# A table of places made row by row: 48 one-row comparisons in place of three broadcast ones

## The chip, the cores and the metric

The kernel runs on one core of one Trainium2 chip. The metric is the device time of one execution in microseconds (us). The core's engines are TensorE (PE; its weight loads are listed as PEld), VectorE (DVE), ScalarE (ACT), GpSimd (POOL) and SyncE (SP), which here only issues transfers.

## What is computed

A batch of 32 images is cut into 36 patches each and embedded; with a class token and 128 text tokens that makes 165 tokens of 256 features per image, 5280 tokens in all. One attention layer with 16 heads follows, then a mixture of experts in which every expert chooses its own tokens:

```python
xn = x_flat * rsqrt(mean(x_flat * x_flat) + EPS) * norm_weight
logits = xn @ router_w.T + router_b
probs = softmax(logits)
gates, idx = top_k(probs.T, cap)          # cap = 5280 / 8 = 660 tokens per expert
hmid = gelu(einsum('ech,efh->ecf', xn[idx], fc1_w) + fc1_b)
ye = einsum('ecf,ehf->ech', hmid, fc2_w) + fc2_b
out = zeros.at[idx].add(ye * gates) / max(gate sums, 1e-9)
```

## The kernel before, in words

The program runs attention over pairs of images (`round_of`), then finds each expert's 660th largest probability by a search on VectorE and ScalarE, numbers the chosen tokens (`POS`, from 0 to 659 per expert, negative where a token is not chosen), and runs the eight experts one after the other. All engines are programmed by hand, each with its own list of instructions; semaphores set the order between them. Within an engine the list is served in order.

**From a mask to a list of token numbers.** For one expert e the chosen tokens' slots lie on 110 partitions in `pos_t`, 48 columns (TPE = 3 groups k of 16). A slot number is split into a tile number a (0 to 5, six tiles of 110) and a place b (0 to 109) within the tile. `slots(e)` (lines 1464 to 1479) makes both: `GE` compares the slot with seven tile edges, `a_t` counts, `INA` is a 0/1 mark of the tile, and `b_t` is the slot less 110 times the tile number. `value_columns` (line 1486) multiplies five value columns (two that make the token number, three that make its weight) by `INA` into `RHS`. `one_hot_places(e, parts)` (lines 1496 to 1504) makes `ONEB`, a table of 48 blocks of 110 numbers in bfloat16: block i of partition p is 1 at the place b_t[p, i] and 0 elsewhere. One part k is 16 blocks. TensorE then multiplies each of the 48 blocks with the matching `RHS` columns and sums them in PSUM (`slot_values`, line 1106; for expert 0 `first_tokens`, line 1087, and `first_weights`, line 1095), which gives the token number and weight of every slot. `tokens(e)` turns that into indices; POOL gathers the rows of those tokens by indirect transfers (line 597).

**One expert on TensorE** (lines 1183 to 1202). `fc1` (line 1142) multiplies in three passes (high and low parts), 16 pieces of 6 matrix multiplications; piece n waits until VectorE has split the hidden piece n-3 (`h_ready`). `fc2` (line 1162) makes four quarters of 24. Between them stand `expert_transposes` (line 1121) of the next expert's gathered rows, `output_rows` (line 1176) and, after fc1's second piece (expert 0: its eighth), `slot_values(e + 1)`, which waits for all of the table: `pe.wait_ge(oh_ready, (NK + 1) * (e + 1))`.

**One expert on VectorE** (`expert`). For expert 0: part 0 of table 1, the low part of hidden piece 2 (`low_hidden`, line 1589), part 1, pieces 3 and 4, part 2, then the rest. For every expert e while e + 2 < 8: after the hidden pieces come the low parts of the next W1 (line 1573), `one_hot_values(e + 2)`, two of `low_xeT(e + 1)` (line 1581), part 0 of table e + 2, `weigh` of three output tiles (line 1567), two more of `low_xeT`, and parts 1 and 2 of table e + 2. Then the next expert's `hidden` begins (lines 1599, 1589, 1602). The table of expert 0 is made ahead of all that, straight after the search. ScalarE makes the hidden pieces (lines 776, 778). POOL scatters weighted rows (line 610).

The table `ONEB` is stored in `H`, `b_t` in an arena (`R_ARENA`) that many short-lived tiles share.

Of the kernel before, what the change touches and what calls it, by code (L numbers as in the profile page):

```python
# [8 lines left out]
BF16 = mybir.dt.bfloat16  # L9
U32 = mybir.dt.uint32  # L10
I32 = mybir.dt.int32
ALU = mybir.AluOpType
# [26 lines left out]
SEG = 128 // NE  # L39
SEGT = NTOK // SEG  # L40
A = 110
# [3 lines left out]
TPE = NK * SEG  # L45
# [80 lines left out]
def build(nc, xT, wl, h0, addrows, clsrows, minus, watt, vecs, rowv, w1, w2, const_f, const_b, out):  # L126
    ctx = ExitStack()
    with ctx:  # L128
        def sb(name, shape, dt=F32):
            return ctx.enter_context(nc.sbuf_tensor(name, shape, dt))  # L130

        def sem(name):
            return ctx.enter_context(nc.semaphore(name))
# [11 lines left out]
        def kb(name):  # L145
            return cb[:, CB[name][0]:CB[name][1]]
# [26 lines left out]
        def cut(arena, *shape, dt=F32):  # L173
            n = int(np.prod(shape))
            words = n if dt == F32 else n // 2
            v = arena[:, at[0]:at[0] + words]
            at[0] += words
            assert at[0] <= arena.shape[1], at[0]
            if dt != F32:
                v = v.bitcast(dt)  # L180
            if len(shape) > 1:
                names = "abcde"[:len(shape)]
                v = v.rearrange(f"p ({' '.join(names)}) -> p {' '.join(names)}", **dict(zip(names, shape)))
            return v

        ONEB = cut(H, TPE, A, dt=BF16)
# [4 lines left out]
        R_ARENA = sb("r_arena", [128, 8576])  # L191
# [23 lines left out]
        GE = cut(R_ARENA, TPE, NA + 1, dt=BF16)  # L215
        INA = cut(R_ARENA, TPE, NA, dt=BF16)
        a_t = cut(R_ARENA, TPE)
        b_t = cut(R_ARENA, TPE, dt=BF16)
        SGN = cut(R_ARENA, ONACT, SEGT)
        at[0] = 4 * 4 * T + 2 * KD * PAIR + KD * T + 3 * RT * D + KD * PAIR  # L220
        VAL = cut(R_ARENA, NCOL, NV + 1, dt=BF16)
        slotv = cut(R_ARENA, NTB, NV, NA)
# [84 lines left out]
        oh_ready, idx_done, tok_chain, tok_ready = [sem(n) for n in ("oh_ready", "idx_done", "tok_chain", "tok_ready")]  # L307
# [316 lines left out]
        def _(act):  # L624
# [112 lines left out]
            for step in range(STEPS):  # L737
# [6 lines left out]
                for c in range(ONACT):  # L744
                    act.activation(SGN[:, c, :], R[:, :], ACT.Sign, bias=here[:, NCAND - ONACT + 1 + c:NCAND - ONACT + 2 + c],
                                   scale=-1.0, accum_out=cnt[:, NCAND - ONACT + c:NCAND - ONACT + c + 1]).then_inc(cnt_act, 1)
# [460 lines left out]
        def _(dve):  # L1207
# [286 lines left out]
                value_columns(e, RHS, 0, NV, oh_ready)  # L1494

            def one_hot_places(e, parts=range(NK)):
                iota = kb("iota")[0:A, :].rearrange("p (o a) -> p o a", o=1).to_broadcast([A, SEG, A])
                if e == 1:
                    dve.wait_ge(idxw_done, 1)
                for k in parts:  # L1500
                    place = b_t[0:A, k * SEG:(k + 1) * SEG].rearrange("p (s o) -> p s o", o=1)\
                        .to_broadcast([A, SEG, A])
                    dve.tensor_tensor(ONEB[0:A, k * SEG:(k + 1) * SEG, :], place, iota, ALU.is_equal)\  # L1503
                       .then_inc(oh_ready, 1)

            def gate_weights():
                link(dve.scalar_tensor_tensor(gate[0:A, :], pos_t[0:A, :], 0.0, pr_t[0:A, :], ALU.is_ge, ALU.mult))
# [97 lines left out]
            def expert(e, u, seen, more):  # L1605

                v = 1 - u
                if e == 0:
                    one_hot_places(1, range(0, 1))
                    low_hidden(0, range(2, 3))  # L1610
                    one_hot_places(1, range(1, 2))
                    low_hidden(0, range(3, 5))
                    one_hot_places(1, range(2, 3))
                    low_hidden(0, range(5, 2 * SV_AT_FIRST + 2))
                    tokens(1)
                    low_hidden(0, range(2 * SV_AT_FIRST + 2, 2 * KFF))
                else:
                    hidden(e, u, seen, range(0, 1))
                    weigh(e - 1, range(3, NA))
                    hidden(e, u, seen, range(1, SV_AT + 1))  # L1620
                    tokens(e + 1)
                    hidden(e, u, seen, range(SV_AT + 1, KFF))
                low_W1(e + 1, v)
                if more:
                    one_hot_values(e + 2)
                low_xeT(e + 1, range(0, 2))
                if more:
                    one_hot_places(e + 2, range(0, 1))
                weigh(e, range(0, 3))
                low_xeT(e + 1, range(2, 4))  # L1630
                if more:
                    one_hot_places(e + 2, range(1, NK))
# [72 lines left out]
```

## Time and profile before

| | |
|---|---|
| runs of the kernel | 847.13, 850.50, 850.14 us; median 850.14 |
| the profiled execution | 851.15 us, of which the span from first to last instruction is 849.4 us |
| granted TensorE clock, mean over the span | 0.927 of full speed |
| TensorE busy | 745.9 us (88%) |
| VectorE busy | 567.9 us (67%), 1343 instructions |
| ScalarE, GpSimd busy | 396.9 us (47%), 378.0 us (45%) |
| span from the search's end to the end | from about 538 us on |

An engine's busy time is the time in which an instruction of it was under way. Durations of consecutive VectorE instructions can overlap: the interval from start to start is then shorter than the duration of one. A merged row of the timeline ("x3") gives the time from the first one's start to the last one's end, so the interval is (that time less one duration) over (count less one). In a chain of waits each row is a stretch on the path that ended last.

### The profile page before, as it was taken

The numbers are of one execution on the slowest core, as the hardware profiler recorded it, in microseconds if no ns is written. First come the engines' busy times: TensorE is split into PE (matmuls) and PEld (weight loads), VectorE is DVE, ScalarE is ACT, GpSimd is POOL, SyncE is SP. The second block draws the span as 40 slices with busy tenths as digits, with TensorE's granted clock in tenths as the row PEclk, the third lists the DMA queues.
The fourth block names the chain that finished last, engine by engine and source line by source line (L and its number), as shares of the span: only waits on it lengthen the run. The fifth ranks groups of instructions, "written<-read, shape, count | busy, mean of one in ns | idle before, by whom it ended". The sixth has DMA issues, their size and how long they took to land. (4 is left out here: it accounts for less than half of the span.)

```text
span 849.4 us, 18757 instructions
## 1 busy us (share of the span) xinstructions
PE 745.9 (88%) x6840; PEld 674.8 (79%) x6840; DVE 567.9 (67%) x1343; ACT 396.9 (47%) x857; POOL 378.0 (45%) x526
## 2 busy tenths in 40 slices
PE   3699999999999999999998521379999999999994
PEld 2577888888888888888887421369999999999994
DVE  1135777677677687677675267785787787877561
ACT  0213454554454554554542247045547466375570
POOL 3113454554554554554543326023636437355334
PEclk8899999999999999999998655569999999999998
DMA  9963666546865666656653161112344443442122
GB/s 297 288 97 47 92 107 93 91 103 98 123 104 97 90 102 99 121 102 97 88 94 74 35 217 64 40 30 82 38 133 79 104 141 53 129 98 35 35 30 32
DMA packets 80687, 82.37 MB, mean 97 GB/s; under 512 B 36161, under 2 KB 74943, under 8 KB 80244
## 3 DMA queue, kind: packets, MB, share of 16 engines
q1 hardware_dynamic: 67980, 66.92, 39.6%
q0 software_dynamic: 11584, 10.96, 8.0%
q10 hardware_dynamic: 1032, 3.30, 1.1%
q8 instruction: 55, 0.90, 0.5%
q14 instruction: 36, 0.29, 0.1%
HBM read 34.59 MB, written 16.22 MB: 60 GB/s over the span
## 5 line engine op out<-in xcount | busy, mean ns | idle before, releaser
L610 POOL DMA_INDIRECT out<-r_arena x48 | 80.3, 1674 | 118.3 <-DVE r_arena L1567 106.3
L523 POOL TENSOR_SCALAR_AFFINE_SELECT r_arena<-r_arena 126x660 f32<-126x660 f32 x128 | 97.0, 768 | 52.6 <-ACT r_arena L671 52.3
L671 ACT ACTIVATE r_arena<-ps_all 126x660 f32<-126x660 f32 x128 | 92.2, 720 | 59.0 <-PE ps_all L899 57.4
L1273 DVE TENSOR_REDUCE mx<-ps_all 128x4 f32<-128x504 f32 (+1 forms) x160 | 105.0, 669 | 16.1 <-PE ps_all L876 14.8
L1284 DVE RECIPROCAL r_arena<-ps_all 128x165 f32<-128x165 f32 x64 | 76.1, 1189 | 57.4 <-PE ps_all L914 57.4
L876 PE MATMUL ps_all<-Kp,Qp 96*65 96x56 f32 (+1 forms) x512 | 91.7, 295 | 0.0
L1589 DVE TENSOR_TENSOR hT_lo<-r_arena,hT_hi 128x330 fp32r<-128x330 f32 x128 | 63.4, 501 | 40.2 <-ACT r_arena L778 39.8
L899 PE MATMUL ps_all<-Qp,Kp 98*126 98x166 f32 x512 | 85.3, 290 | 4.4 <-ACT r_arena L671 2.9
L597 POOL DMA_INDIRECT xe<-xn_rows,r_arena x48 | 59.5, 1240 | 59.7 <-issue 35.7
L776 ACT ACTIVATE hT_hi<-ps_all,vec_s 128x330 fp32r<-128x330 f32 x128 | 68.9, 538 | 35.9 <-PE ps_all L1142 33.8
L1142 PE MATMUL ps_all<-xeT_hi,W_hi 128*128 128x330 f32 x256 | 83.4, 326 | 1.1 <-DVE xeT_lo L1581 1.1
L1142 PE MATMUL ps_all<-xeT_lo,W_hi 128*128 128x330 f32 x256 | 82.7, 323 | 0.0
L649 ACT ACTIVATE q_hi<-ps_all,vec_s 128x166 fp32r<-128x166 f32 x64 | 22.0, 395 | 129.6 <-PE ps_all L837 129.6
L1142 PE MATMUL ps_all<-xeT_hi,W_lo 128*128 128x330 f32 x256 | 82.1, 321 | 0.0
L1162 PE MATMUL ps_all<-hT_hi,W_hi 128*128 128x330 f32 x256 | 81.7, 319 | 0.0
L1162 PE MATMUL ps_all<-hT_hi,W_lo 128*128 128x330 f32 x256 | 80.8, 315 | 0.0
L1162 PE MATMUL ps_all<-hT_lo,W_hi 128*128 128x330 f32 x256 | 80.4, 314 | 0.0
L899 PEld LDWEIGHTS ps_all<-Qp,Kp 98*126 98x126 f32 x512 | 69.7, 192 | 10.4 <-ACT r_arena L671 6.4
L876 PEld LDWEIGHTS ps_all<-Kp,Qp 96*65 96x65 f32 (+1 forms) x512 | 67.9, 168 | 5.6
L778 ACT ACTIVATE r_arena<-ps_all,vec_s 128x330 f32<-128x330 f32 x128 | 68.0, 532 | 0.0
L914 PE MATMUL ps_all<-r_arena,V 126*32 126x165 f32 x1024 | 61.6, 313 | 1.1 <-POOL r_arena L523 1.0
L914 PE MATMUL ps_all<-r_arena,cf 126*32 126x165 f32 x1024 | 60.2, 307 | 0.0
(178 smaller groups left out, 1703.7 us busy)
## 6 DMA issues: line engine op xcount, KB each, us to landing
H<-w SPq DMA_DIRECT2D x16, 1024.0 KB, 6.0
Qp<-q_hi SPq DMA_DIRECT2D x64, 166.0 KB, 3.9
Kp<-k_hi SPq DMA_DIRECT2D x128, 63.0 KB, 4.2
Qp<-q_lo SPq DMA_DIRECT2D x32, 166.0 KB, 4.7
out<-H SPq DMA_DIRECT2D x16, 330.0 KB
xn_rows<-r_arena SPq DMA_DIRECT2D x16, 330.0 KB
Kp<-k_lo SPq DMA_DIRECT2D x64, 63.0 KB, 4.1
H<-h SPq DMA_DIRECT2D x1, 3360.0 KB, 25.5
```

The source lines that it names most:

```text
L523: pool.affine_select(PT[0:S, g, :, :], PT[0:S, g, :, :], [[0, 4], [STEP - 1, T]], ALU.is_ge, 0.0, base=STEP - 2, channel_multiplier=-STEP) ...
L610: pool.indirect_dma_start(rows_out, bass.IndirectOffsetOnAxis(tok[0:A, e % NTB, a:a + 1], 0), yw[0:A, a, :], None, bounds_check=NTOK - 1, ...
L671: act.activation(PT[0:S, g, :, :].rearrange("p (k h) t -> p k h t", k=2), pair[:, :, :, 0:T], ACT.Exp, scale=float(HD) ** -0.5).then_inc(e ...
L776: act.activation(hT_hi[:, f, j * HALF:(j + 1) * HALF], bank(n % 4)[:, 0:HALF], ACT.Gelu, bias=b1_s[:, e, f:f + 1]).then_inc(gelu_done, 1)
L778: act.activation(h_raw[:, n % 4, :], bank(n % 4)[:, 0:HALF], ACT.Gelu, bias=b1_s[:, e, f:f + 1]).then_inc(gelu_done, 1)
L876: mm = pe.matmul(dst[0:rows, 2 * j * cols:2 * (j + 1) * cols].rearrange("p (w s) -> p w s", w=2), Qp[0:MROW, q, h, at_row:at_row + rows], ...
L899: mm = pe.matmul(dst[0:S, j * TE:(j + 1) * TE], Kp[0:MROW + 2, q, h, g % 2, :], Qp[0:MROW + 2, q, h, :], start=(j == 0), stop=(j == 1), sk ...
L914: mm = pe.matmul(dst, lhs, PT[0:S, 2 * c + w, j, :], start=(w == 0 and part == 0), stop=(w == 1), skip_group_check=True)
L1142: mm = pe.matmul(bank(n % 4)[:, 0:HALF], w[:, k, f * 128:(f + 1) * 128], x[:, k, cols], start=(i == 0), stop=(i == len(terms) - 1))
L1162: mm = pe.matmul(bank(4 + c)[:, 0:HALF], w[:, f, c * 128:(c + 1) * 128], h[:, f, cols], start=(i == 0), stop=(i == len(terms) - 1))
L1273: dve.tensor_reduce(dst, src, AX.X, ALU.max).then_inc(max_ready, 1)
L1284: dve.reciprocal(rS[:, c, :], bank(2 + c)[:, T:2 * T]).then_inc(rs_sum, 1)
```

## The change

`one_hot_places` issues, for each block i, one `tensor_scalar` over 110 numbers that compares the row 0 to 109 with the number in `b_t[:, i]` of each partition (a per-partition scalar operand), in place of one `tensor_tensor` per part over 16 blocks, in which both the places and the row 0 to 109 are spread by a step of 0. The semaphore is raised by the last of each 16. `b_t` becomes float32, and it is cut from the arena after `SGN` instead of before.

```diff
         a_t = cut(R_ARENA, TPE)
-        b_t = cut(R_ARENA, TPE, dt=BF16)
         SGN = cut(R_ARENA, ONACT, SEGT)
+        b_t = cut(R_ARENA, TPE)
@@
             def one_hot_places(e, parts=range(NK)):
-                iota = kb("iota")[0:A, :].rearrange("p (o a) -> p o a", o=1).to_broadcast([A, SEG, A])
                 if e == 1:
                     dve.wait_ge(idxw_done, 1)
                 for k in parts:
-                    place = b_t[0:A, k * SEG:(k + 1) * SEG].rearrange("p (s o) -> p s o", o=1)\
-                        .to_broadcast([A, SEG, A])
-                    dve.tensor_tensor(ONEB[0:A, k * SEG:(k + 1) * SEG, :], place, iota, ALU.is_equal)\
-                       .then_inc(oh_ready, 1)
+                    for i in range(k * SEG, (k + 1) * SEG):
+                        ins = dve.tensor_scalar(ONEB[0:A, i, :], kb("iota")[0:A, :], b_t[0:A, i:i + 1], None, ALU.is_equal)
+                    ins.then_inc(oh_ready, 1)
```

## Rows read from the trace of the kernel before

**Rows 1.** Chain of waits, experts 0 and 1: start us, us, what.

```profile
570.09 0.44 ACT r_arena L778
570.55 0.50 DVE hT_lo L1589
571.06 1.91 DVE H L1503
573.01 2.69 PE ps_all L1106 x48
...
603.51 2.41 PE ps_all L1106 x48
605.92 12.88 PE ps_all L1142 x84
```

**Rows 2.** TensorE's waits after 573 us: waiter, released by: us, times, longest.

```profile
PE ps_all L1106 <- DVE H L1503: 0.9, 1, 0.9
```

**Rows 3.** The table's line by itself: duration ns min/median/max, first and last start.

```profile
L1503 DVE TENSOR_TENSOR H<-r_arena,cb x24: 1979/1982/1991, 540.9 to 771.7; 110x1760 bf16<-110x1760 bf16 x24
```

**Rows 4.** Timeline, table of expert 0: start us, us, engine, line, operation.

```profile
540.86 5.79 DVE L1503 TENSOR_TENSOR H<-r_arena,cb 110x1760 bf16<-110x1760 bf16 x3
546.70 1.66 PE L1087 MATMUL ps_all<-RHS,H 110*110 110x12 bf16 x16 [0.25 <-DVE H L1503]
```

**Rows 5.** Timeline of VectorE, table of expert 1.

```profile
565.64 1.99 DVE L1503 TENSOR_TENSOR H<-r_arena,cb 110x1760 bf16<-110x1760 bf16 x1
567.69 0.50 DVE L1589 TENSOR_TENSOR hT_lo<-r_arena,hT_hi 128x330 fp32r<-128x330 f32 x1
568.11 1.99 DVE L1503 TENSOR_TENSOR H<-r_arena,cb 110x1760 bf16<-110x1760 bf16 x1
570.01 1.04 DVE L1589 TENSOR_TENSOR hT_lo<-r_arena,hT_hi 128x330 fp32r<-128x330 f32 x2
```

**Rows 6.** Timeline, table of expert 2 and TensorE's pass over it.

```profile
593.66 1.98 DVE L1503 TENSOR_TENSOR H<-r_arena,cb 110x1760 bf16<-110x1760 bf16 x1
596.61 1.27 DVE L1567 TENSOR_SCALAR r_arena<-ps_all,r_arena 110x256 f32<-110x256 f32 x3 [0.96 <-PE ps_all L1176]
598.61 3.88 DVE L1503 TENSOR_TENSOR H<-r_arena,cb 110x1760 bf16<-110x1760 bf16 x2
...
603.35 2.57 PE L1106 MATMUL ps_all<-RHS,H 110*110 110x30 bf16 x48
```

**Rows 7.** VectorE rows for the fixed part of an instruction, without and with a per-partition scalar.

```profile
26.16 0.33 DVE L1313 COPY bvB<-vec_s 128x110 f32<-128x110 f32 x2
...
L1313 DVE COPY bvB<-vec_s 128x110 f32<-128x110 f32 x2 | 0.3, 208 | 0.0
...
528.42 0.55 DVE L1388 TENSOR_SCALAR_CACHE_REDUCE r_arena<-r_arena,cand 128x330 f32<-128x330 f32 x1
...
528.89 0.55 DVE L1388 TENSOR_SCALAR_CACHE_REDUCE r_arena<-r_arena,cand 128x330 f32<-128x330 f32 x1
...
L1567 DVE TENSOR_SCALAR r_arena<-ps_all,r_arena 110x256 f32<-110x256 f32 x48 | 20.2, 477 | 21.9 <-PE ps_all L1176 14.1 <-issue 7.8
```

**Rows 8.** VectorE rows for the rate: elements per cycle.

```profile
L1455 DVE TENSOR_SCALAR r_arena<-r_arena 128x330 f32<-128x330 f32 x1 | 0.3, 333 | 0.0
L1454 DVE TENSOR_TENSOR r_arena<-r_arena 128x330 f32<-128x330 f32 x1 | 0.5, 502 | 0.0
...
L1474 DVE TENSOR_TENSOR r_arena<-r_arena 110x288 bf16<-110x288 bf16 x8 | 2.6, 324 | 0.0
```

**Rows 9.** Windows: us, engines' busy time, PEclk, DMA share, GB/s.

```profile
572.08:575.40 3.32, 2.39 (x48) 2.39 (x48) 2.12 (x4) 1.17 (x3) 0.00 (x0) 1.00 0.00 0
575.40:578.80 3.40, 3.40 (x17) 3.40 (x16) 0.06 (x1) 0.96 (x2) 0.00 (x0) 0.50 0.00 0
...
592.00:838.00 246.00, 245.37 (x1856) 244.65 (x1855) 181.12 (x403) 140.86 (x295) 120.17 (x81) 1.00 0.36 80
```

**Rows 10.** A VectorE copy beside GpSimd's transfers: duration ns min/median/max.

```profile
L1599 DVE CAST W_hi<-H x56: 280/286/389, 602.4 to 821.9; 128x256 fp32r<-128x256 f32 x56
```

## The prediction, made before the changed kernel was run

> **What bounds the kernel now.** I read the chain of waits first, in order of time, for the stretch in which the table is used, then TensorE's list of waits, then the timelines around the table. From 573 us to 837 us the chain is TensorE alone, pass after pass, with one wait by the list [rows 2]: 0.9 us before the pass over the table of expert 1. Ahead of it stands VectorE's last part of that table [rows 1]. So the 21 parts for experts 1 to 7 cost the kernel nothing but that wait, while the three for expert 0, made with TensorE idle, lie on the path in full. The table takes 24 instructions of 1.98 us [rows 3]. What matters is, first, whether 16 one-row comparisons are shorter or longer than one broadcast one, and second, how much room the table has before TensorE wants it.
>
> **Interval of the old instruction.** Three parts take 5.79 us, one lasts 1.98 us: (5.79 - 1.98) / 2 = 1.905 us from start to start [rows 3, 4]. Per element VectorE takes (1982 - 502) / (1760 - 330) = 1.035, say 1.04 ns at one element per cycle [rows 3, 8]; 1760 elements are 1830 ns, so 75 ns of the interval are fixed and the broadcast form runs at one element per cycle.
>
> **Interval of the new one.** It has two terms, and neither shape is in the trace.
>
> Fixed part. Without a per-partition scalar it is 65 to 75 ns: two copies of 110 elements take 0.33 us, one lasts 208 ns, so 122 ns from start to start, less 57 ns for 110 elements at two per cycle [rows 7]. With such a scalar, two quite different instructions give the same larger value: L1388 starts every 0.47 us with 330 elements (470 - 343 = 127 ns), and three L1567 take 1.27 us with one of 477 ns, so 396 ns each, less 256 x 1.04 = 266 ns, is 130 ns [rows 6, 7]. The scalar costs some 60 ns that the preceding instruction doesn't hide. Bounds: 65 and 130 ns. I take 130, since it is what both rows with a scalar show; neither row is exactly of this form (one also reads out an accumulator, the other reads PSUM).
>
> Streaming part. A float32 `tensor_scalar` within SBUF lasts 333 ns where the two-source one of the same 330 elements lasts 502: 169 ns less, half of the 343, so two per cycle [rows 8]. Two 16-bit sources of 288 elements last 324 ns, which is 150 ns fixed and 174 ns of streaming, near two per cycle too [rows 8]. The new instruction has one source within SBUF and 16-bit elements on both sides, so both doublings should apply: 110 x 1.04 / 4 = 29 ns. Bounds: 29 ns, 57 ns at two per cycle, 115 ns at one.
>
> I take 130 + 29 = 159 ns from start to start, and 211 + 29 = 240 ns for the duration (L1567 has 477 - 266 = 211 ns outside its stream). Sixteen take 16 x 0.159 = 2.54 us against 1.905. Each part is 0.64 us longer: the stream shrinks from 1.83 to 0.46 us, but the fixed parts grow from 0.075 to 2.08 us.
>
> The Trainium skill, Vector Engine (DVE) Microarchitecture Reference, section Measured stream behaviour on trn2, speaks against this: built-in ops pay about 75 ns per instruction after queue overlap, and it names no extra for a scalar. By that rule sixteen would take 16 x (75 + 29) ns = 1.66 us and the change would gain a little; the rows agree with 75 ns for instructions without such a scalar and have 127 to 130 for those with one.
>
> **Where it lands, place by place.**
>
> Expert 0's table. Before, it begins at 540.86 us and ends at 546.65. After, the last of 48 ends at 540.86 + 47 x 0.159 + 0.24 = 548.57: **+1.9 us**, all on the path; TensorE's pass over each part (1.66 us) stays shorter than a part and only the last shows [rows 4].
>
> Expert 1's table. Part 0 starts at 565.64 and ends its turn at 568.18 instead of 567.55; hidden piece 2 was ready at about 567.69, so part 1 starts at 568.60 instead of 568.11, ends its turn at 571.14, pieces 3 and 4 take 2 x 0.42 us (before they waited for ScalarE, whose rows end at 570.53), and part 2 runs from 571.98 to 571.98 + 15 x 0.159 + 0.24 = 574.60 instead of 572.96 [rows 1, 5]. TensorE waits for exactly this: **+1.6 us**, and its idle stretch grows from 0.9 to about 2.6 us. The hidden pieces behind part 2 are late as well, but they are wanted after a table pass of 2.4 us.
>
> Tables of experts 2 to 7 (six times the same pattern, 34.2 us apart; the first is in the rows). Part 0 starts at 593.66 and would end at 596.2; `weigh` behind it waits for TensorE until 596.61 anyway, so that one is free (0.96 us idle before, 0.3 after). Parts 1 and 2 start at 598.61; the last of 32 ends at 598.61 + 31 x 0.159 + 0.24 = 603.78, and TensorE wants the table at 603.35 [rows 6]. With 0.05 us for the signal that is a new wait of 0.48 us, six times: **+2.9 us**. The point from which this begins is an interval of (603.35 - 0.05 - 0.24 - 598.61) / 31 = 0.144 us; the cover of 0.9 us is used up. Queued behind on VectorE are the W2 split, hidden pieces 0 and 1 and `weigh` of three more tiles: 1.3 us late, but the hidden piece that VectorE needs next comes only after TensorE's table pass of 2.4 us [rows 1], so it catches up, and fc1 wants none of these rows before that pass is over.
>
> Everything else. The number of semaphore raises stays; TensorE's passes read the same bytes; `b_t` as float32 is 48 elements of one short instruction per expert, made well ahead: nothing.
>
> **TensorE's clock.** After its wait of 0.93 us and its pass over the table the granted clock was 0.50 for 3.40 us, that is 1.2 instead of 2.4 GHz, and those 3.4 us did the work of 1.7: 1.7 us lost. In the 246 us after, where the same pass comes without a wait, the clock stays at 1.00 [rows 9]. The change lengthens the first wait and puts a shorter one (0.48 us) in front of six other passes. Bounds: no further fall, or one at each of the seven, 0 to 11.9 us. New waits are half as long as the one that was followed by a fall, so I take one further fall: **+1.7 us**.
>
> **The sum.** 1.9 + 1.6 + 2.9 + 1.7 = 8.1 us. The profiled execution took 851.15 us (span 849.4), so it would take 859.3. It lies 1.0 us above the median of the runs, 850.14, on which I put the forecast: **858.3 us**.
>
> **GpSimd.** Its indirect transfers run beside the table. The Trainium skill, SBUF — State Buffer, in its part on ports, says that a VectorE instruction in a two-port mode keeps GpSimd out of SBUF for its whole length, and that whichever comes first holds up the other. A two-per-cycle copy runs 56 times in this stretch, some beside such transfers, and lasts 280 to 389 ns with a median of 286 [rows 10], so the trace shows at most 0.1 us for one of 56: I put it at zero.
>
> **The rivals.**
>
> A, the scalar is free (chance 0.14). The interval is 70 + 29 = 99 ns, 1.58 us per part. Expert 0's table then waits for TensorE's own passes (three of 1.66 us) and gains 0.8 us; expert 1's part 2 still starts at 570.97, held by ScalarE, and gains 0.3; the rest is covered. 850.1 - 1.1 = 849.0 us, no slower than before. For it: every row without a scalar. Against it: both rows with one. It decides below 119 ns (1.905 / 16).
>
> B, the faster stream fails by half (0.12). Two elements per cycle, because only one of the doublings applies. Interval 187 ns, duration 270: +3.3, +3.0 and six waits of 1.4 us, 14.8 us in all: 864.9 us. No row has both doublings at once. At one per cycle (0.04) the interval is 245 ns: +6.1, +5.8, part 0 delays `weigh` by 1.0 us, and six waits of 4.2 us give 37 us: 887 us.
>
> C, the clock (0.10). The waits come out as forecast, but the clock falls behind nearly each: 6.4 + 6 x 1.7 = 16.6, 866.7 us. For it: the one fall behind a wait; against it: the new waits are half as long.
>
> **How the numbers follow.** The forecast has 0.60, and by itself a range of 852 to 862: 852 if the interval is just under the 0.144 us at which the six waits go, 862 with three falls. The range for 8 in 10 leaves out A and the one-per-cycle case: 851 to 867. Half a percent, 4.25 us, is about what a measurement here can tell from no change: slower than 854.4 are B, C and nearly all of the forecast, 0.80; within it A and the forecast's low end, 0.18; faster by more, 0.02.
>
> **What would show it.** In the changed kernel's trace: 384 one-row comparisons of about 240 ns (180 with no price for the scalar, 268 at two per cycle), merged groups of 16 or 32 that take 0.159 us each; TensorE's first pass over expert 1's table about 3.5 us later than before; in its list of waits, seven on the table, one of 2.6 us and six of 0.5; the clock row after 592 us below 1.00 if there were falls. The forecast is wrong if the interval is below 0.144 us or the six waits are missing.

## The result and the profile after

The changed kernel takes 861.47 us (median of 4 runs, 861.01 to 861.66) against 850.07 for the kernel before on the same chip: 1.015 times as long, 95% interval 1.012 to 1.018, so 11.4 us slower. Forecast were 858.3 us and a range of 851 to 867. Measured again on another chip (below) it was 865.07 against 848.44, so 16.6 us slower.

The profiled execution has a span of 859.9 us. The table's line, by itself and in the timeline; columns as in [rows 3] and [rows 4 to 6].

```profile
L1501 DVE TENSOR_SCALAR H<-cb,r_arena x384: 233/246/610, 536.8 to 784.4; 110x110 bf16<-110x110 bf16 x192
...
564.09 2.64 DVE L1501 TENSOR_SCALAR H<-cb,r_arena 110x110 bf16<-110x110 bf16 x16 [0.29 <-DVE r_arena L1536]
566.65 0.50 DVE L1587 TENSOR_TENSOR hT_lo<-r_arena,hT_hi 128x330 fp32r<-128x330 f32 x1
567.06 2.64 DVE L1501 TENSOR_SCALAR H<-cb,r_arena 110x110 bf16<-110x110 bf16 x16
569.61 0.90 DVE L1587 TENSOR_TENSOR hT_lo<-r_arena,hT_hi 128x330 fp32r<-128x330 f32 x2
570.43 2.63 DVE L1501 TENSOR_SCALAR H<-cb,r_arena 110x110 bf16<-110x110 bf16 x16
...
595.29 2.63 DVE L1501 TENSOR_SCALAR H<-cb,r_arena 110x110 bf16<-110x110 bf16 x16
598.23 1.27 DVE L1565 TENSOR_SCALAR r_arena<-ps_all,r_arena 110x256 f32<-110x256 f32 x3 [0.30 <-PE ps_all L1176]
...
600.23 5.24 DVE L1501 TENSOR_SCALAR H<-cb,r_arena 110x110 bf16<-110x110 bf16 x32
```

(2.64 - 0.246) / 15 is 0.160 us from start to start, so a part takes 2.55 us instead of 1.905. Part 0 of table 2 still ends ahead of the weighing (L1565), which waits 0.30 us where it waited 0.96 [rows 6]; parts 1 and 2 end 5.24 us after their start instead of 3.88.

TensorE's list of waits from 573 us on, where before there was one of 0.9 us [rows 2]:

```profile
PE ps_all L1106 <- DVE H L1501: 4.2, 7, 1.8
```

The longest of the seven stands in front of the pass over table 1. Some microseconds ahead of it TensorE waits once more, for a hidden piece:

```profile
570.16 0.42 PE L1142 MATMUL ps_all<-xeT_hi,W_hi 128*128 128x330 f32 x1 [0.79 <-DVE hT_lo L1587]
...
573.12 3.91 PE L1106 MATMUL ps_all<-RHS,H 110*110 110x30 bf16 x48 [1.79 <-DVE H L1501]
```

The chain of waits over two experts:

```profile
636.64 3.29 DVE H L1501 x21
639.95 1.85 DVE H L1501 x11
641.80 0.04 issue
641.85 2.61 PE ps_all L1106 x48
644.46 13.09 PE ps_all L1142 x84
...
674.94 1.94 DVE H L1501 x11
676.93 2.61 PE ps_all L1106 x48
679.54 14.42 PE ps_all L1142 x84
```

Before, the chain was TensorE alone in this stretch and fc1's 84 multiplications took 12.88 us [rows 1]. Now VectorE's table is on it in each of the six experts, and fc1 behind the pass takes 13.1 and 14.4 us in turn. The 14.4 us are the clock's doing: it is low for part of the stretch behind the first, third and fifth pass, 0.63 of full speed on the mean of the window below; the windows (columns as in [rows 9]) show it behind the pass over table 2 and not behind that over table 3:

```profile
609.00:612.50 3.50, 3.50 (x17) 3.50 (x17) 0.50 (x1) 1.82 (x4) 2.89 (x3) 0.63 0.39 37
644.30:657.40 13.10, 13.10 (x89) 12.91 (x88) 9.30 (x30) 11.50 (x26) 10.62 (x8) 1.00 0.37 61
```

**Where the time went.** The stage begins with VectorE's copy of the slots (line 1459). Attention and search ahead of it are untouched, but vary from run to run: over the thirteen traces of this study the copy starts between 532.3 and 540.6 us. So the cleaner comparison is from that copy to the end of the span. It is still one execution of each kernel, and the clock in expert 0 differs between executions by up to 2.7 us (see e6). The kernel before:

```profile
L1459 DVE COPY r_arena<-ps_all x1: 558/558/558, 538.2 to 538.2; 110x384 f32<-110x384 f32 x1
```

The changed one:

```profile
L1459 DVE COPY r_arena<-ps_all x1: 558/558/558, 534.1 to 534.1; 110x384 f32<-110x384 f32 x1
```

From there it is 849.4 - 538.2 = 311.2 us before and 859.9 - 534.1 = 325.8 after: 14.6 us more. In these two executions the part ahead of the stage was 4.1 us shorter in the changed kernel, so that the spans differ by 10.5 only; the medians differ by 11.4, on the second chip by 16.6. The 14.6 us, from milestone to milestone:

| from | to | before | after | more |
|---|---|---|---|---|
| copy of the slots | token numbers of expert 0 | 10.2 | 12.1 | 1.9 |
| token numbers of expert 0 | pass over table 1 | 24.6 | 26.9 | 2.3 |
| pass over table 1 | pass over table 2 | 30.3 | 32.4 | 2.1 |
| five times: pass to next pass | | 171.2 | 179.2 | 8.0 |
| pass over table 7 | end | 74.9 | 75.2 | 0.3 |

### The profile page after: what moved, and what is told of

The parts are those of the page before. It is cut to its first block and busy times, and to the rows that moved or that the text cites. A ratio compares the mean times of both kernels' runs of the same rounds, so it can differ in the third digit from the quotient of the medians.

```text
span 859.9 us, 19117 instructions
## 1 busy us (share of the span) xinstructions
PE 749.4 (87%) x6840; PEld 677.1 (79%) x6840; DVE 583.2 (68%) x1703; ACT 398.0 (46%) x857; POOL 374.6 (44%) x526
## 5 line engine op out<-in xcount | busy, mean ns | idle before, releaser
L610 POOL DMA_INDIRECT out<-r_arena x48 | 77.1, 1606 | 127.4 <-DVE r_arena L1565 115.4
L1273 DVE TENSOR_REDUCE mx<-ps_all 128x4 f32<-128x504 f32 (+1 forms) x160 | 104.8, 668 | 15.4 <-PE ps_all L876 14.1
L1142 PE MATMUL ps_all<-xeT_hi,W_hi 128*128 128x330 f32 x256 | 86.0, 336 | 1.9 <-DVE xeT_lo L1579 1.1
L1142 PE MATMUL ps_all<-xeT_lo,W_hi 128*128 128x330 f32 x256 | 85.0, 332 | 0.0
L1142 PE MATMUL ps_all<-xeT_hi,W_lo 128*128 128x330 f32 x256 | 84.4, 330 | 0.0
L1501 DVE TENSOR_SCALAR H<-cb,r_arena 110x110 bf16<-110x110 bf16 x384 | 63.0, 268 | 0.3 <-DVE r_arena L1536 0.3
```

Source lines behind the costliest of these rows:

```text
L610: pool.indirect_dma_start(rows_out, bass.IndirectOffsetOnAxis(tok[0:A, e % NTB, a:a + 1], 0), yw[0:A, a, :], None, bounds_check=NTOK - 1, ...
L1142: mm = pe.matmul(bank(n % 4)[:, 0:HALF], w[:, k, f * 128:(f + 1) * 128], x[:, k, cols], start=(i == 0), stop=(i == len(terms) - 1))
L1273: dve.tensor_reduce(dst, src, AX.X, ALU.max).then_inc(max_ready, 1)
L1501: ins = dve.tensor_scalar(ONEB[0:A, i, :], kb("iota")[0:A, :], b_t[0:A, i:i + 1], None, ALU.is_equal)
```

## The experiments

Each time stands against the kernel before, run on the same chip (its medians there: 848.21 us for e1 to e4, 848.44 for e5 to e8, 849.07 for e9 to e11). e1 is not in the table: its own time, 859.82 us, says nothing. "Stage" is the length from the copy of the slots to the end in the profiled execution, 311.2 us for the kernel before.

| kernel | median us | ratio, 95% interval | stage us |
|---|---|---|---|
| e2, table 0 by rows | 850.94 | 1.0029 (0.9998 to 1.0060) | 313.7 |
| e6, table 1 by rows | 852.34 | 1.0053 (1.0029 to 1.0077) | 317.1 |
| e3, tables 2 to 7 by rows | 855.96 | 1.0094 (1.0061 to 1.0127) | 320.0 |
| e4, two of three parts of tables 2 to 7 | 849.41 | 0.9997 (0.9975 to 1.0019) | 311.1 |
| e5, the change again | 865.07 | 1.0198 (1.0157 to 1.0240) | 326.9 |
| e7, the change, SV_AT 2 | 857.22 | 1.0088 (1.0053 to 1.0124) | 319.4 |
| e9, broadcast form, tables 2 to 7 delayed | 857.70 | 1.0093 (1.0067 to 1.0119) | 322.0 |
| e11, the change, SV_AT 2 and SV_AT_FIRST 5 | 854.05 | 1.0053 (1.0016 to 1.0090) | 314.4 |
| e10, the kernel before, SV_AT_FIRST 5 | 846.97 | 0.9971 (0.9949 to 0.9993) | 309.3 |
| e8, table in pairs | 922.42 | 1.0865 (1.0828 to 1.0902) | 386.0 |

**e1, series of single instructions.**

```diff
+for i in range(16): tensor_scalar(ONEB[:, i], row, a_t[:, i:i+1], is_equal)          # 1
+for i in range(16): tensor_scalar(ONEB[:, i], row, 5.0, is_equal)                    # 2
+for i in range(8):  tensor_scalar(sgn[i*A:(i+1)*A], ones[0:A], a_t[:, i:i+1], is_equal)   # 3, float32
+for i in range(4):  tensor_scalar(flat[880 numbers], cb[0:880], a_t[:, i:i+1], is_equal)  # 4
+for i in range(4):  tensor_scalar(flat[880 numbers], cb[0:880], 5.0, is_equal)       # 5
+for i in (1, 2):    tensor_tensor(cells(i), b_t spread over 110 rows of 16, cells(0), is_equal)  # 6
```

> The kernel before, with series of instructions put in between the search and the first table, where VectorE works alone; they write scratch, and the whole run is longer by their sum (about 16 us), so its time says nothing. Series 1: 16 one-row comparisons of 110 bf16 with a float32 scalar per partition. Series 2: the same with a constant in the instruction. Series 3: 8 of 110 float32 with a scalar per partition. Series 4 and 5: 4 of 880 bf16, with a scalar per partition and with a constant. Series 6: 2 two-source comparisons of 1760 bf16 in which the innermost step of both sources is one. Theory 'the scalar per partition costs 60 ns, the stream runs at four per cycle': from start to start 160, 100, 190, 360 and 300 ns in series 1 to 5. Rival 'fixed part of 100 ns plus two per cycle, and the scalar is free': 160, 160, 160, 560 and 560 ns. Series 6: 0.99 us if two per cycle, 1.9 us if one.

The timeline of VectorE, and below it each line's durations in ns (min/median/max):

```profile
535.68 2.63 DVE L1641 TENSOR_SCALAR H<-cb,r_arena 110x110 bf16<-110x110 bf16 x16
538.35 1.67 DVE L1644 TENSOR_SCALAR H<-cb 110x110 bf16<-110x110 bf16 x16
540.05 1.58 DVE L1647 TENSOR_SCALAR r_arena<-cf,r_arena 110x110 f32<-110x110 f32 x8
541.67 1.52 DVE L1650 TENSOR_SCALAR H<-cb,r_arena 110x880 bf16<-110x880 bf16 x4
543.23 1.28 DVE L1653 TENSOR_SCALAR H<-cb 110x880 bf16<-110x880 bf16 x4
544.55 2.06 DVE L1656 TENSOR_TENSOR H<-r_arena,H 110x1760 bf16<-110x1760 bf16 x2
...
L1641 DVE TENSOR_SCALAR H<-cb,r_arena x16: 241/244/253, 535.7 to 538.1; 110x110 bf16<-110x110 bf16 x16
L1644 DVE TENSOR_SCALAR H<-cb x16: 186/188/195, 538.4 to 539.8; 110x110 bf16<-110x110 bf16 x16
L1650 DVE TENSOR_SCALAR H<-cb,r_arena x4: 444/444/449, 541.7 to 542.8; 110x880 bf16<-110x880 bf16 x4
```

Series 1 starts every (2.63 - 0.244) / 15 = 159 ns, series 2 every (1.67 - 0.188) / 15 = 99: the scalar per partition costs 60 ns of the engine's time. Series 4 starts every (1.52 - 0.444) / 3 = 359 ns; 770 elements more take 200 ns more than in series 1, 0.26 ns each, so the stream does run at four per cycle. Series 3 and 5 start every 187 and 300 ns (by their lines' medians of 271 and 381 ns). The theory is right on all six; the rival meets only series 1. (The sum was overestimated: 11 us, not 16.) The Trainium skill's 75 ns per instruction (Vector Engine (DVE) Microarchitecture Reference, Measured stream behaviour on trn2) is met by series 2, 99 - 29 = 70 ns; series 1 has 130, which that page doesn't mention. Series 6 starts every 2.06 - 1.07 = 0.99 us: the two-source comparison runs at two per cycle once no innermost step is 0.

**e2, table 0 alone; e6, table 1 alone; e3, tables 2 to 7 alone.** In each, a table is made by rows or as before:

```diff
+            def by_rows(e, k):
+                return e == 0            # e6: e == 1; e3: e >= 2
...
+                    if by_rows(e, k):
+                        for i in range(k * SEG, (k + 1) * SEG):
+                            ins = dve.tensor_scalar(ONEB[0:A, i, :], kb("iota")[0:A, :], b_r[0:A, i:i + 1], None, ALU.is_equal)
+                        ins.then_inc(oh_ready, 1)
+                        continue
```

> Only the table of expert 0 by rows, all others in the broadcast form. Theory 'each table costs what the chain says': table 0 lies on the path in full, +1.9 us over the kernel before, about 852, plus or minus a change of the clock in expert 0. Rival 'the loss of 11 us is set off by the late start of expert 0 (other clock, other order of transfers)': most of the 11 us comes with this alone, about 860.

> Only the table of expert 1 by rows. Theory: TensorE's wait in front of this table grows by 1.6 us, and the clock falls for longer after it (up to 1.7 us): +1.6 to +3.5 us. Rival 'the hidden pieces behind the table hold up TensorE too': a second wait behind the table pass, +4 us or more.

> Only the tables of experts 2 to 7 by rows, those of 0 and 1 in the broadcast form. Theory 'six waits in front of the table pass, and what the clock makes of them': six waits of 0.4 to 0.5 us (2.9 us) and two or three falls of the clock (1.4 us each), in all +6 to +8 us, about 857. Rival 'the steady part costs only its waits': +3 us, 853.

Measured +2.7, +3.9 and +7.8 us by the medians, +2.5, +5.9 and +8.8 by the stage. The rival that the late start of expert 0 sets off everything is out: table 0 alone gives 2.7 us. So is e6's rival: no wait for a hidden piece stands behind the pass over table 1.

Of the 5.9 us of e6's stage, 2.7 arise ahead of the first row comparison. The clock stood at 0.50 all the way from expert 0's token numbers to that comparison, and TensorE's 48 multiplications for expert 0's weights took 4.42 us instead of 2.40. The chain and the window of e6, then the chain of the kernel before:

```profile
557.42 4.42 PE ps_all L1096 x48
542.50:562.40 19.90, 11.11 (x75) 10.72 (x76) 14.40 (x34) 3.49 (x8) 6.95 (x6) 0.50 0.12 34
```

```profile
562.59 2.40 PE ps_all L1095 x48
```

In the kernel before the clock had risen by then (0.68 on the mean from 556.0 to 565.6 us). From the token numbers to the start of table 1 it is 19.9 us in e6 and 17.3 in the kernel before, although nothing there is by rows. The trace of e9, whose table 1 is in the broadcast form, has the same: its pass over table 1 starts 2.7 us later after the token numbers. Why the clock rises late in some executions is open. Without these 2.7 us table 1 costs 3.2 by the stage, within the theory's 1.6 to 3.5, and the median's interval (2.5 to 6.5 us) doesn't speak against it. The three parts then add up to 2.5 + 3.2 + 8.8 = 14.5 us, against 14.6 for the whole change.

Of the 3.2 us, 1.7 are the later start of the pass (its wait is 1.8 us instead of 0.93). The other 1.5 lie behind it, where the clock is low for longer, as the windows from the start of the pass over table 1 show. The kernel with table 1 by rows:

```profile
571.49:574.99 3.50, 3.50 (x47) 3.50 (x47) 1.17 (x3) 0.00 (x0) 0.00 (x0) 0.65 0.00 0
574.99:586.49 11.50, 11.50 (x66) 11.50 (x66) 4.69 (x13) 8.20 (x17) 3.47 (x4) 0.81 0.08 22
```

The kernel before:

```profile
573.01:576.51 3.50, 3.50 (x52) 3.50 (x52) 1.19 (x3) 0.24 (x1) 0.00 (x0) 0.84 0.00 0
576.51:588.01 11.50, 11.50 (x70) 11.50 (x70) 5.81 (x15) 9.31 (x18) 4.45 (x4) 0.90 0.11 32
```

That is (0.35 x 3.5 + 0.19 x 11.5) - (0.16 x 3.5 + 0.10 x 11.5) = 1.7 us of full-speed work lost more.

TensorE's list of waits of the kernel with tables 2 to 7 by rows:

```profile
PE ps_all L1107 <- DVE H L1507: 2.4, 6, 0.5
```

Six waits of 0.4 us make 2.4 us. In its chain the clock falls behind three of the six passes, as many as in both traces of the change, but not the same ones: here behind the first, second and fifth.

**e4, two of three parts by rows.**

```diff
-                return e >= 2
+                return e >= 2 and k < 2
```

> In the tables of experts 2 to 7, parts 0 and 1 by rows and part 2 broadcast; tables 0 and 1 broadcast. 192 of the 384 one-row comparisons are there. Theory 'there is cover for 0.9 us behind the weighing and for 0.96 us ahead of it': part 0 is 0.65 us later and hidden, part 1 is 0.65 us later and hidden, so no wait of TensorE on these tables, no fall of the clock after 592 us, and the time of the kernel before, 850. Rival 'every one-row comparison costs its share wherever it stands' (by contention on VectorE's side): half of the loss, 855.

849.41 us, 0.9997 of the kernel before. The timeline of VectorE and TensorE's list of waits over experts 1 to 7:

```profile
593.54 1.27 DVE L1576 TENSOR_SCALAR r_arena<-ps_all,r_arena 110x256 f32<-110x256 f32 x3 [0.29 <-PE ps_all L1177]
...
595.54 2.68 DVE L1507 TENSOR_SCALAR H<-cb,r_arena 110x110 bf16<-110x110 bf16 x16
598.14 1.98 DVE L1512 TENSOR_TENSOR H<-r_arena,cb 110x1760 bf16<-110x1760 f32 x1
...
PE ps_all L1107 <- DVE H L1512: 0.9, 1, 0.9
```

192 one-row comparisons, which cost VectorE 12 x 0.65 = 7.8 us more, cost the kernel nothing: the only wait left is that on table 1. So the row form costs nothing where there is cover for it; a second late part in a row has none.

**e9, no row form, only the delay.**

```diff
+                    if e >= 2 and k == 2:
+                        dve.tensor_tensor(idle, b_t[0:11] spread, iota spread, ALU.is_equal)   # 1210 elements of scratch
                     place = b_t[0:A, k * SEG:(k + 1) * SEG]
```

> The kernel before, all tables in the broadcast form; in the tables of experts 2 to 7 a scratch comparison of 1210 elements stands in front of part 2, so that parts 1 and 2 end 1.3 us later, as they do by rows. No one-row comparison is in it. Theory 'the loss of tables 2 to 7 comes from when the table is ready, and from the clock that falls behind the wait': six waits of 0.4 to 0.5 us, two or three falls of the clock after 592 us, and the time of the kernel with only these tables by rows, +8 us, 856. Rival 'it comes from the one-row comparisons themselves, from two-port accesses against GpSimd for one': +3 us or less, 851.

857.70 against 849.07 us: +8.6, where the row form of the same tables costs 7.8. (2.7 us of its stage in the table above stand ahead of table 1's pass, see e6.) This is the test that settles the steady part: the loss comes from when the table is ready. TensorE's waits in it, table 1's among them:

```profile
PE ps_all L1106 <- DVE H L1509: 3.1, 7, 1.0
```

That is some 2.1 us in the six, and again three falls of the clock, behind the first, second and fifth pass.

**e5, the change again; e7, the pass over the table later; e11, both passes later.**

```diff
-SV_AT, SV_AT_FIRST = 1, 4
+SV_AT, SV_AT_FIRST = 2, 4            # e7; e11: 2, 5
```

> The changed kernel once more, for its time beside the kernel before on this chip and a second look at where its clock falls. If the losses add up (table 0, table 1, tables 2 to 7): 2.5 + about 2.5 + 8 = 13 us over the kernel before. Rival 'they share something, so that the sum is less': 8 to 10 us.

> The changed kernel with SV_AT 2 instead of 1: from expert 1 on TensorE takes the table pass two pieces of fc1 later, so 1.8 us more cover; VectorE reads the pass's result one round of hidden pieces later. All 384 comparisons stay by rows. Theory 'the eight us of tables 2 to 7 come from the waits in front of the pass': the six waits go, no fall of the clock after expert 1, and about 8 us come back: 4 to 5 us over the kernel before. Rival 'they come from VectorE being busier everywhere': at most 3 us come back.

> The changed kernel with SV_AT 2 and SV_AT_FIRST 5: both passes two pieces later. With SV_AT 2 alone it took 857.2 us, 8.8 over the kernel before. Theory 'the fast form of the table is late for expert 1 by 2.6 us, of which 1.8 us can be covered': 2 to 4 us less than with SV_AT 2 alone, 853 to 855. Rival 'the wait only moves behind the hidden pieces': 857.

e5 takes 16.6 us more than the kernel before, 15.7 by the stage: more than the 13 of its theory and far more than the rival's 8 to 10. Its waits and its falls of the clock in experts 1 to 7 are those of the first trace of the change.

e7 has all 384 row comparisons and takes 857.22 us, 7.85 less than the unaltered change on the same chip. TensorE's list of waits from 580 us on holds no table any more, and the windows show no fall over experts 1 to 7:

```profile
PE ps_all L1176 <- ACT yS L787: 0.6, 1, 0.6
...
592.00:838.00 246.00, 246.00 (x1855) 244.34 (x1854) 197.13 (x682) 141.71 (x295) 121.61 (x81) 1.00 0.38 82
```

So the eight us come back as the theory had it, but not down to 4 to 5 us over the kernel before: 8.8 remain, 8.2 by the stage. Expert 0 has 6.9 of the 8.2: table 0 makes 1.9, the pass over table 1 starts 2.8 later after the token numbers, and 2.2 more are lost behind it, with the clock at 0.53 for 8.8 us from the start of the pass. The rest are stalls of about 0.2 us per expert, in which fc1 waits for hidden pieces: the passes lie 34.42 us apart instead of 34.23. The theory had too little for the clock in expert 0 and nothing for the stalls.

e11 stands at 1.0053 where e7 has 1.0088. That is the theory's 853 to 855 us, but the two intervals overlap, and its four runs spread from 849.3 to 857.8. Its trace agrees: no table is waited for, TensorE waits 2.1 us for hidden pieces instead, one short fall of the clock is left in expert 0, and its stage is 3.2 us above the kernel before.

**e10, the kernel before with its first pass later.**

> The kernel before with SV_AT_FIRST 5 instead of 4: in expert 0 TensorE takes the pass over table 1 two pieces of fc1 later. Theory 'its wait of 0.93 us and the fall of the clock behind it are worth 0.9 + 1.7 us': -1 to -2.6 us. Rival 'piece 9 then waits for hidden piece 5, which VectorE makes behind the table': the wait only moves, no change.

846.97 against 849.07 us, 0.9971 (0.9949 to 0.9993): slightly faster than the kernel before, by 2.1 us where the theory had 1 to 2.6. The wait of 0.9 us on table 1 is gone, one of 0.4 on a hidden piece has come, and the second fall of the clock in expert 0 doesn't appear; TensorE's list of waits:

```profile
PE ps_all L1142 <- DVE hT_lo L1589: 0.4, 1, 0.4
```

**e8, the table in pairs.**

```diff
-        ONEB = cut(H, TPE, A, dt=BF16)
+        ONEB = cut(H, NK, A, SEG, dt=BF16)
...
-    mm = pe.matmul(..., ONEB[0:A, i, :], ...)
+    mm = pe.matmul(..., ONEB[0:A, i // SEG, :, i % SEG], ...)
...
+    place = b_t[0:A, k * SEG:(k + 1) * SEG] spread over 110 rows of 16
+    dve.tensor_tensor(ONEB[0:A, k], place, iota_s[0:A], ALU.is_equal).then_inc(oh_ready, 1)
```

> The kernel before with the table laid out as place, then block (blocks innermost): three two-source comparisons of 1760 per table as before, but the innermost step of the places is one, and the row 0 to 109 is written out once, 16 times each, by GpSimd while it is idle. TensorE reads its weights at a step of 16. Theory 'one step of 0 in the innermost place kept the broadcast form at one element per cycle': a comparison starts every 0.99 us instead of 1.905; table 0 gains 1.4 us (TensorE's passes of 1.66 us at the low clock set it then), table 1 gains 0.9 us and leaves no wait in front of TensorE's pass, tables 2 to 7 nothing: 2.3 us less, and up to 1.7 more if the fall of the clock behind the wait goes too. Rival 'TensorE loads stepped weights more slowly': the pass over the table grows from 2.4 us, eight times and on the path, slower than before.

The VectorE half is right and the whole is a bad miss: 922.42 us, 74 more. The three comparisons of table 0 in the timeline, then the pass over table 2 in the chain of waits, and the windows over the experts:

```profile
538.45 3.04 DVE L1506 TENSOR_TENSOR H<-r_arena,iota_s 110x1760 bf16<-110x1760 bf16 x3
...
619.81 9.73 PE ps_all L1109 x48
629.54 14.58 PE ps_all L1145 x84
...
592.00:838.00 246.00, 246.00 (x1503) 245.68 (x1502) 143.78 (x341) 116.13 (x240) 99.64 (x69) 0.89 0.32 75
```

The table takes 3.04 us instead of 5.79 [rows 4]. But 48 multiplications with stepped weights take 9.73 us where they took 2.41 [rows 1], and the clock is 0.89 on the average. Seven such passes make 51 us of the 74. Behind the six over tables 2 to 7 fc1 took 14.1 to 15.6 us instead of 12.9, 12 us more together, and no wait stands in front of these passes: the clock falls there without one. The other 11 us I haven't taken apart. The rival had the mechanism; I had no figure for it.

## Why the prediction was right

**The interval: right.** Forecast 159 ns, measured 160 in the change and 159 alone; the duration 240 ns, measured 246. The pieces, 130 ns fixed with a scalar, 70 without, and four per cycle, are each shown by e1. Rival A, whose interval of 99 ns is exactly that of the comparison with a constant, is out, and so is rival B with its 187 ns.

**Table 0: right.** 1.9 us forecast, 1.9 in the trace, 2.7 (interval 0 to 5) by e2's median.

**Table 1: the wait right in kind, short in size.** Forecast +1.6 us; the pass starts 2.3 us later counted from expert 0's token numbers. The 0.7 us between them stand ahead of the table. TensorE's fc1 and transposes in front of it took 0.4 us longer, with the clock low for longer. The other 0.3 is a gap in front of part 0 of table 1, which the trace ascribes to nothing but the instruction before it. It is not the row form's: e2, with table 1 broadcast, has it too, and e6, with table 1 by rows, has not. The timeline of e2:

```profile
570.90 1.99 DVE L1512 TENSOR_TENSOR H<-r_arena,cb 110x1760 bf16<-110x1760 bf16 x1 [0.27 <-DVE r_arena L1547]
```

The idle time in front of the pass is 1.8 us, not 2.6, because TensorE had already waited 0.8 us for hidden piece 3 before its piece 7 of fc1 (both counted from 0; piece n needs the first n - 3 hidden pieces, the last of which is number n - 4). The prediction's account of table 1 left that wait out. It changes where TensorE idles, not when the pass starts.

**Tables 2 to 7: right in kind, 0.7 us short.** Forecast six waits of 0.48 us, 2.9 in all. Found: six waits that the list gives with 2.4 us. From pass to pass one costs 0.85 us where the clock does not fall (676.93 - 641.85 = 35.08, less 34.23): the pass starts 0.6 us later, and fc1 behind it takes 0.2 more in one stall (last section). Six times 0.6 are 3.6 us. That the threshold lies between one and two late parts is shown by e4, and by e9 that lateness alone does it.

**The clock: the mis-sized term.** I took one further fall, 1.7 us, and gave 0.10 to the case that it falls behind nearly each. It fell behind three of the six new waits, with about 1.5 us each (14.42 less the 12.88 of [rows 1]), and stayed low longer behind table 1, 1.7 us by the windows. So this term is 4.6 + 1.7 = 6.3 us instead of 1.7. With it the steps give 1.9 + 2.3 + 3.6 + 6.3 = 14.1 us; three stalls of fc1 make 0.6 more, together 14.7 against the stage's 14.6. The reason for taking one fall was that the new waits were half as long as the one that was followed by a fall. That reason fails: in e3, e9 and both traces of the change a wait of 0.4 us was followed by a fall three times of six, and in e4 and e7, without the wait, never. Why it is three of six, and in the change every second one, is open.

**The forecast's position within the noise.** The part ahead of the table moves by some us from run to run in either kernel (from 532.3 to 540.6 us in the traces), so 858.3 against 861.47 is as much luck as size. By the stage the forecast of 8.1 us is short by 6.5: 4.6 of that are the clock, 0.7 each the start of table 1 and the six waits, 0.6 the stalls. Rival C, with 16.6 us and 866.7, is nearer to the stage's 14.6 and to the 865.07 us of the second chip than the forecast is; what happened lies between the two, nearer to C.

## What to carry to other kernels

An operand with an innermost step of 0 costs the fast mode, but cutting the instruction until the step is gone pays only if elements per instruction are many beside the fixed part: here 110 elements save 86 ns of stream (29 instead of 115) and cost 130 ns of fixed part, 60 of them for the scalar per partition, where the broadcast form pays 75 ns once for 16 blocks. An engine that is idle a third of the time can still be exactly on time for one consumer; look for the cover in front of each consumer (here 0.96 and 0.9 us), since e4 put 7.8 us of work into it for nothing, and the third part by rows, 3.9 us more, cost 8. And a short wait of TensorE can cost more than its length by the clock behind it: 2.4 us of waits came with 4.6 us lost to the low clock.

## What the runs showed that I had not expected

**VectorE's conversions slow down beside GpSimd's transfers.** I put this at zero. In three of the six experts of the change, VectorE's conversions are shifted onto GpSimd's indirect transfers, and two that take 0.17 and 0.28 us otherwise take 0.45 and 0.51, while the two-source instruction ahead of them keeps its 0.17. Timeline of VectorE, then of GpSimd:

```profile
648.84 0.17 DVE L1554 TENSOR_TENSOR r_arena<-r_arena 110x6 f32<-110x6 f32 x1
648.92 0.45 DVE L1556 CAST r_arena<-r_arena 110x6 int32<-110x6 f32 x1
648.99 0.51 DVE L1597 CAST W_hi<-H 128x256 fp32r<-128x256 f32 x1
```

```profile
648.26 1.62 POOL L610 DMA_INDIRECT out<-r_arena  x1 [0.30 <-issue]
```

This is what the Trainium skill says (SBUF — State Buffer, on ports: whichever comes first holds up the other). The trace agrees in kind, with a price of 0.2 to 0.3 us, but the conversions end at 649.5 us at the latest and the transfer's record only at 649.9. Behind them hidden piece 3 was late and one weight load of fc1 came after 0.37 instead of 0.15 us. Of the 384 row comparisons the longest took 610 ns, where in e1, with GpSimd idle, none took over 253; yet the run of 32 took 5.24 us against the 5.17 of the forecast. That it was GpSimd is read from the overlap in time only; no run kept GpSimd away.

**Stepped weights.** Weights read at a step of 16 two-byte elements make a multiplication of 110 rows come every 203 ns (9.73 / 48) instead of 50 (2.41 / 48), part of it at the low clock (0.66 on the mean of the pass over table 2).
